# Context-by-weight products in f16 parts, with one power of two for a whole batch

## The reference

```
q  = layernorm(x)
t  = Wt @ ctx ; p = Wp @ q ; g = Wg @ ctx            (each 256 x 512)
att = sum over each of 8 groups of 32 channels of p * g, times 0.125
v  = groupnorm(Wz (att * t)) * gamma + beta + ctx
x1 = x + v
gate, up = fp4(layernorm(x1)) @ fp4(w_gate).T, ... @ fp4(w_up).T     (512 -> 1408)
out = x1 + fp4(silu(gate) * up) @ fp4(w_down).T
```

## Time and profile before

| what | us |
|---|---|
| median of 3 runs | 1733.88 |
| lowest and highest | 1733.24, 1734.05 |
| the profiled execution's own time | 1733.28 |
| its span in the profile | 1731.4 |
| PE busy | 1677.1 (97%) |
| DVE busy | 1501.5 (87%) |
| ACT busy | 825.9 (48%) |
| POOL busy | 722.5 (42%) |

### The profile page before, as it was taken

The page is one execution under the profiler, slowest core; times in us unless marked ns, Lnnn a source line. Parts: engine busy times, 40 slices in busy tenths (PEclk is TensorE's granted clock), DMA queues, the critical chain, the costliest instruction groups (busy, mean ns, idle before and its releaser), DMA issues.

```text
span 1731.4 us, 27880 instructions
## 1 busy us (share of the span) xinstructions
PE 1677.1 (97%) x8723; PEld 922.2 (53%) x8723; DVE 1501.5 (87%) x2577; ACT 825.9 (48%) x1472; POOL 722.5 (42%) x951
## 2 busy tenths in 40 slices
PE   2799999999999999999999999999999999999999
PEld 1665555555555555555555555555555555555544
DVE  7877888889888888988888898888888988888887
ACT  3665544544445444444545444454544445445422
POOL 7986343334444333444433334443333444433310
PEclk9999999999999999999999999999999999999999
DMA  8123334343434344343334434333434444343322
GB/s 258 34 43 81 83 91 95 88 100 89 95 81 94 89 91 99 88 106 76 88 89 100 94 85 104 76 89 91 103 88 94 95 82 92 91 94 88 76 50 49
DMA packets 412150, 155.86 MB, mean 90 GB/s; under 512 B 383200, under 2 KB 384480, under 8 KB 412128
## 3 DMA queue, kind: packets, MB, share of 16 engines
q1 hardware_dynamic: 396352, 125.17, 33.9%
q10 hardware_dynamic: 15776, 30.41, 5.5%
HBM read 43.03 MB, written 16.78 MB: 35 GB/s over the span
## 4 chain that ended last, share of the span: by engine, by line
PE 91%; POOL 6%; DVE 1%; DMA 1%; issue 1%; ACT 0%; SPq 0%; POOLq 0%; DVEq 0%; ACTq 0%
PE pairs L550 52%; PE work L561 26%; PE work L500 5%; PE work L512 3%; PE work L527 2%; PE ubank L527 2%; POOL raw L1864 2%; POOL raw L1853 1%; POOL w_parts L1864 1%; POOL w_parts L1853 1%; DMA raw<-in_L_ffn_w_gate 0%; DMA hT_parts<-raw 0%; POOL xc L1787 0%; PE pairs L580 0%; POOL q_parts L1803 0%
## 5 line engine op out<-in xcount | busy, mean ns | idle before, releaser
L550 PE MATMUL pairs<-w_gate_hi,xT_parts 128*128 128x512 f16 (+1 forms) x1536 | 555.1, 361 | 0.5 <-DMA xT_parts<-raw 0.5
L550 PE MATMUL pairs<-w_up_hi,xT_parts 128*128 128x512 f16 (+1 forms) x1536 | 554.7, 361 | 0.0
L561 PE MATMUL work<-w_parts,hT_parts 128*128 128x512 f16 x2079 | 458.9, 379 | 0.9 <-DMA hT_parts<-raw 0.9
L561 PEld LDWEIGHTS work<-w_parts,hT_parts 128*128 128x128 f16 x2079 | 203.5, 99 | 236.0 <-issue 1.1
L550 PE MATMUL pairs<-w_up_lo,xT_parts 128*128 128x512 f16 (+1 forms) x768 | 277.5, 361 | 0.0
L550 PE MATMUL pairs<-w_gate_lo,xT_parts 128*128 128x512 f16 (+1 forms) x768 | 277.4, 361 | 0.0
L550 PEld LDWEIGHTS pairs<-w_gate_hi,xT_parts 128*128 128x128 f16 x1536 | 152.7, 99 | 155.7 <-issue 8.2
L550 PEld LDWEIGHTS pairs<-w_up_hi,xT_parts 128*128 128x128 f16 x1536 | 150.3, 98 | 146.8
L964 ACT ACTIVATE early<-pairs,w_unit 128x512 f32<-128x512 f32 (+1 forms) x192 | 124.8, 650 | 163.2 <-PE pairs L550 163.2
L915 ACT ACTIVATE wm<-h 128x1408 bf16<-128x1408 f32 (+2 forms) x65 | 87.2, 1341 | 204.9 <-DVE h L1184 204.9
L873 ACT CAST raw<-hq 128x704 f16<-128x704 f32 x126 | 98.2, 779 | 180.0 <-DVE hq L1201 179.3
(11 more groups left out here) (193 smaller groups left out, 2801.7 us busy)
## 6 DMA issues: line engine op xcount, KB each, us to landing
out<-raw SPq DMA_DIRECT2D x64, 256.0 KB, 2.1
c_in<-in_ctx ACTq DMA_DIRECT2D x29, 512.0 KB, 3.8
x_in<-in_x ACTq DMA_DIRECT2D x29, 512.0 KB, 5.2
raw<-in_L_ffn_w_down SPq DMA_DIRECT2D x2, 1408.0 KB, 8.8
raw<-in_L_ffn_w_gate SPq DMA_DIRECT2D x2, 1280.0 KB, 8.5
w_parts<-in_L_ffn_w_up SPq DMA_DIRECT2D x2, 1280.0 KB, 9.2
x_in<-in_x SPq DMA_DIRECT2D x3, 512.0 KB, 4.1
c_in<-in_ctx SPq DMA_DIRECT2D x3, 512.0 KB, 4.7
```

Of the source, the lines that this page charges most:

```text
L550: mm = pe.matmul(pairs[:, pair, n, 0:b - a], xT[s][part][:, k, :], w1[n][wpart][:, k, a:b], start=(k == 0 and part == 0 and wpart == 0), s ...
L561: mm = pe.matmul(obank[:, :], hT[part][:, k, :], w2[wpart][:, k, :], start=(k == 0 and part == 0 and wpart == 0), stop=(k == KH - 1 and pa ...
```

## The change

The context gets one power of two for the whole batch in place of one for each row, so that the same f16 parts serve `gram` and `u_rows`; the 32-bit parts go, and the fused weight is split into f16 parts as well. The power of u is taken out in `copy_u`.

- `ctx_square` writes its squares to another buffer. The row sums go to DRAM (`save_rows`) and come back with all 256 of them on every partition (`spread_rows`), both issued by ACT. `ctx_peak` (DVE) takes their largest. For batch 0 the peak goes over TensorE (`attention_rows`, `attention_top`, `attention_spread`), together with that of the weight.
- `ctx_fit` makes four passes (f16 and f32 for each tile), `ctx_lo` (POOL) subtracts the f16 from the f32 and writes f16. `ctx_hi` and `ctx_fit_lo` go.
- `scale_of_u` (DVE) makes the factor for `copy_u`.
- In the body, ACT does `ctx_fit` behind `affine(i+1,0)`, DVE does `ctx_peak` behind `gated(j,0,1)` and `ctx_power` and `scale_of_u` behind `gated(j,0,2)` (before: `ctx_power` ahead of `gated(j,0,0)`), POOL does `ctx_root` behind `columns` and both `ctx_lo` behind `columns_affine`.

```diff
-        wuT = [sb(f"wuT_{part}", [P, HT, C], F32R) for part in ("hi", "lo")]
+        wuT = [sb(f"wuT_{part}", [P, HT, C], F16) for part in ("hi", "lo")]
@@ PE, u_rows
-                pe.wait_ge(c_ready, HT * b + HT)
+                pe.wait_ge(c_fit_ready, HT * b + HT)
-                        mm = pe.matmul(u_bank(b, s), wuT[wpart][:, k, s * P:(s + 1) * P], c_wide[part][:, k, :],
+                        mm = pe.matmul(u_bank(b, s), wuT[wpart][:, k, s * P:(s + 1) * P], c_parts[:, k, part, :],
@@ PE, before turn_weights(0)
             top_of_rows(0)
+            attention_rows()
             spread_top(0)
+            attention_spread()
@@ ACT
+                act.wait_ge(u_scale_made, b + 1)
+                nc.scalar.activation(u_sb[:, s, :], u_bank(b, s), ACT.Identity, scale=u_scale[:, 0:1],
...
+            def save_rows(b):
+                act.wait_ge(c_squared, HT * b + HT)
+                at_least(act, c_rows_spread, 16 * (b - 1))
+                nc.scalar.dma_start(c_rows, c_norm[:, 0, :]).then_inc(c_rows_saved, 16)
+            def spread_rows(b):
+                act.wait_ge(c_rows_saved, 16 * b)
+                at_least(act, c_peaked, b)
+                nc.scalar.dma_start(c_all[:], c_rows.rearrange("p h -> (p h)").unsqueeze(0).to_broadcast([P, HT * P])
+                                    ).then_inc(c_rows_spread, 16)
...
                 for s in range(HT):
                     nc.scalar.activation(c_parts[:, s, 0, :], c_in[:, s, :], ACT.Identity,
-                                         scale=c_norm[:, 2, s:s + 1]).then_inc(c_fit_done, 1)
+                                         scale=c_norm[:, 2, 0:1]).then_inc(c_fit_done, 1)
+                    nc.scalar.activation(c_scaled[:, s, :], c_in[:, s, :], ACT.Identity,
+                                         scale=c_norm[:, 2, 0:1]).then_inc(c_scaled_done, 1)
@@ ACT, body
                     ctx_square(i + 2)
+                    save_rows(i + 2)
                 h_hi(j - 1, 0)
                 h_hi(j - 1, 1)
                 silu_group(j, 0, 0)
+                if ahead:
+                    spread_rows(i + 2)
...
-                if ahead:
-                    ctx_fit(i + 2)
                 silu_group(j, 0, 1)
                 x_hi(j + 1)
-                if ahead:
-                    ctx_hi(i + 2)
                 silu_group(j, 0, 2)
                 if more:
                     affine(i + 1, 0)
                 if ahead:
-                    ctx_fit_lo(i + 2)
+                    ctx_fit(i + 2)
@@ DVE
+            def ctx_peak(b):
+                if isinstance(b, int) and b == 0:
+                    dve.wait_ge(att_spread, 1)
+                    nc.vector.tensor_copy(c_norm[:, 1, 1:2], mixed_bank(0)[:, 1:2]).then_inc(c_peaked, 1)
+                    return
+                dve.wait_ge(c_rows_spread, 16 * b)
+                at_least(dve, c_floored, b)
+                nc.vector.tensor_reduce(c_norm[:, 1, 1:2], c_all[:, :], AX_X, ALU.max).then_inc(c_peaked, 1)
@@ DVE, start: order
+            attention_peak()
             weight_top(0)
+            attention_top()
             weight_max(1, 0)
             normalise1(0, 1)
             weight_unit(0)
+            ctx_peak(0)
+            weight_max(1, 1)
             ctx_power(0)
...
             copy_group(0)
+            ctx_peak(1)
             ctx_power(1)
@@ DVE, body
                     ln1_moments(i + 2, 0)
-                    ctx_power(i + 2)
                 gated(j, 0, 0)
...
                 gated(j, 0, 1)
                 if ahead:
+                    ctx_peak(i + 2)
                     ln1_moments(i + 2, 1)
...
                 gated(j, 0, 2)
+                if ahead:
+                    ctx_power(i + 2)
+                    scale_of_u(i + 2)
                 h_first(j)
@@ POOL
-                pool.wait_ge(c_squared, HT * b + HT)
+                pool.wait_ge(c_peaked, b + 1)
...
-                nc.gpsimd.tensor_tensor(c_wide[1][:, s, :], c_in[:, s, :], c_wide[0][:, s, :].bitcast(F32),
-                                        ALU.subtract).then_inc(c_ready, 1)
+                nc.gpsimd.tensor_tensor(c_parts[:, s, 1, :], c_scaled[:, s, :], c_parts[:, s, 0, :],
+                                        ALU.subtract).then_inc(c_fit_ready, 1)
@@ POOL, body
+                columns(i + 1)
                 if ahead:
                     ctx_root(i + 2)
-                columns(i + 1)
+                columns_affine(i + 1)
                 if ahead:
                     ctx_lo(i + 2, 0)
-                columns_affine(i + 1)
-                if ahead:
                     ctx_lo(i + 2, 1)
```

More of the change, by code:

```diff
@@ L137, in build @@
         cT = sb("cT", [P, HT, 2, KD, P], F16)
-        c_wide = [sb(f"c_{part}", [P, HT, D], F32R) for part in ("hi", "lo")]
+        c_scaled = sb("c_scaled", [P, HT, D])
+        c_all = sb("c_all", [P, HT * P])
+        u_scale = sb("u_scale", [P, 1])
         c_norm = sb("c_norm", [P, 4, HT])
@@ L620, in spread_top, with attention_rows, attention_spread @@
                           stop=True).then_inc(w_allmax_done, 1)
+            def attention_rows():
+                pe.wait_ge(wu_peaked, 1)
+                pe.wait_ge(c_squared, HT)
+                for n, column in enumerate((wu_pow[:, 0:1], c_norm[:, 0, 0:1], c_norm[:, 0, 1:2])):
+                    mm = pe.matmul(mixed_bank(0)[0:1, n * P:(n + 1) * P], column, ident[:, :], start=True, stop=True)
+                mm.then_inc(att_rows_done, 1)
+            def attention_spread():
+                pe.wait_ge(att_top_done, 2)
+                pe.matmul(mixed_bank(0)[:, 0:2], ones_row[:, :], att_top[:, 0:2], start=True,
+                          stop=True).then_inc(att_spread, 1)
             def unit_read(m):
@@ L886, in ctx_fit @@
                 at_least(act, gram_done, b)
+                at_least(act, c_turned, 16 * b)
+                at_least(act, u_done, HT * b)
+                act.wait_ge(c_squared, HT * b + HT)
                 for s in range(HT):
                     nc.scalar.activation(c_parts[:, s, 0, :], c_in[:, s, :], ACT.Identity,
[L889 to L904 removed]
+                                         scale=c_norm[:, 2, 0:1]).then_inc(c_fit_done, 1)
+                    nc.scalar.activation(c_scaled[:, s, :], c_in[:, s, :], ACT.Identity,
+                                         scale=c_norm[:, 2, 0:1]).then_inc(c_scaled_done, 1)
             def q_hi(b):
@@ L993, in _ @@
             ctx_square(1)
+            save_rows(1)
             weights_lo(0)
             weights_lo(1)
+            spread_rows(1)
             weights_hi(2)
@@ L1025, in _ @@
             weights_hi(11)
-            ctx_hi(1)
             weights_hi(12)
@@ L1049, in _ @@
             weights_hi(19)
-            ctx_fit_lo(1)
             weight_grain(9)
@@ L1088, in _ @@
             ctx_square(2)
+            save_rows(2)
             affine(1, 0)
+            spread_rows(2)
             weights_lo(31)
@@ L1099, in _ @@
             ctx_fit(2)
-            ctx_hi(2)
             q_hi(2)
@@ L1103, in _ @@
             grain_x(2)
-            ctx_fit_lo(2)
             silu_group(1, 1, 2)
@@ L1497, in _ @@
             weight_unit(0)
+            ctx_peak(0)
+            weight_max(1, 1)
             ctx_power(0)
-            weight_max(1, 1)
+            attention_parts()
+            scale_of_u(0)
             weight_round(0)
+            attention_lo()
             weight_scales(1, 0)
@@ L1517, in _ @@
             variance(0)
+            scale_of_u(1)
             ln1_moments(1, 1)
@@ L1586, in _ @@
             h_lo(0, 0)
+            ctx_peak(2)
             ctx_power(2)
+            scale_of_u(2)
             x_scales(2)
```

98 lines of the change are left out of this document (67 added, 31 removed).

## The result

The changed kernel takes **1769.93 us** (median of 6 runs, 1768.74 to 1771.30) against 1733.97 of the kernel before on the same chip (6 runs, 1733.24 to 1734.93). The ratio is 1.0209, with an interval of 1.0198 to 1.0220. The forecast was 1771.6. Every time here is the median of the executions at the usual granted clock, 0.996 to 0.999; the one execution that fell to 0.756 (2224.82 us, in run 4) is left out. The profiled execution took 1770.55 with a span of 1768.5 us, 37.1 more than the 1731.4 before.

A forecast was written before the change was run, and what follows sets the result against it. PE's own work was taken to bound the loop, the POOL chain the part before it. Loop +32.5, last body -0.3 and start +5.5 gave +37.7 on the median 1733.9: 1771.6 us, range 1738 to 1798.

The forecast's parts named there:

- the loop: 29 rounds that prepare a batch ahead: PE stall less saved matmul time, net +1.12 us a round, 32.5 us.
- the start: Before the loop: POOL waits 3.3 us for the first peak, 2.2 more for the second; 5.5 us, from 2 to 8.
- The PE work that goes: Twelve u matmuls a batch at L527 with f16 operands: 0.33 us saved a batch, bounds 0.20 to 0.42.
- a switch less on the way into L550: Behind the u matmuls on PE: one switch fewer, counted into the 0.33 us saved a batch.
- The shift of DVE: DVE's chain to `gated(j+1,1,0)`: 1.8 us later at 808.5 through added instructions and `ctx_lo` port collisions, bounds 0.3 to 2.6.
- The stall of PE: PE in each loop round: waits 1.8 - 0.35 = 1.45 us for DVE's late results.
- both named deadlines: PE's `hidden(j+1,1,2)` needs `gated(j+1,1,0)`, room 0.5 us; `output(j)` needs h's transpose, room 0.35 us.
- The trip through DRAM: ACT's `save_rows` and `spread_rows`: 2.1 us to landing, no wait; taken as zero, other end 1 us a round.
- Rival (c): `save_rows` lands over 4 us after issue, ACT's chain moves, up to 1 us more a round: 1800; chance 0.05.
- (a): Port costs DVE's chain nothing, shift under 0.35 us, the matmul saving stays: 1729.5 or 1726; chance 0.13.
- (b): Only one `ctx_lo` collides; shift about 0.8 us, PE waits 0.45 a round: 1743; chance 0.12.
- (d): f16 u matmuls no faster than the old form, stalls as forecast, 9.9 us more: 1781; chance 0.03 within the forecast's range.

The follow-up runs named there:

- run 4: Kernel before the change, only the u product taking f16 operands, the scaling left out and squares in another buffer: 1726.59 us, ratio 0.9958.
- run 2: Changed kernel in its own order; in the loop POOL's `ctx_lo` subtracts 2 columns instead of 512: 1736.98 us, ratio 1.0016 to the kernel before.
- run 3: Kernel before the change, only `ctx_hi` moved behind `affine(i+1,0)` and `ctx_lo(0)` behind `columns_affine`, no instruction added: 1757.52 us, ratio 1.0133.
- run 11: Changed kernel with early context passes in the loop and three reorderings before it, measured once more on another chip: 1731.35 us, ratio 0.9988.
- Run 7: Changed kernel with early context passes in the loop, and ACT's `ctx_fit(1)` split into two pairs behind `weights_lo(8)`: 1735.52 us, ratio 1.0007.
- run 8: Changed kernel, early context passes; before the loop `ctx_peak(1)`, `weight_max(1,0)`, `ctx_peak(0)` earlier on DVE and `ctx_fit(1)` split on ACT: 1730.89 us, ratio 0.9983.
- run 1: Changed kernel, loop reordered: `ctx_fit` ahead of `silu_group(j,0,2)`, both `ctx_lo` ahead of `columns_affine`, root, peak and power passes earlier: 1737.11 us, ratio 1.0018.

## Why the prediction was right, and where it was not

The sign, the place and the mechanism held, and the time came out 1.7 us from the forecast. But that closeness is owed to two errors of opposite sign: the loop was forecast at 32.5 us and cost 29 x 0.946 = 27.4; the start was forecast at 5.5 and cost 37.1 - 27.4 + 0.1 = 9.8.

**The PE work that goes: 0.22 us a batch, not 0.33.** The pitch of 0.2155 was right. What failed is the step "the first takes 0.42 us because its 32-bit weight load lies open behind the L512 ones". The 0.19 us at the first matmul are gone, but the 32-bit block ahead grew by 0.18 us, though its operands are the same; why, no run shows. The 0.03 us for "a switch less on the way into L550" had no row behind it and did not show either. Only the difference of pitch was saved, near the stated lower bound of 0.20. Run 4 gives the same 0.22. Read from the u block alone, the saving would be 0.40; only both blocks together, from the start of the one ahead, show what PE gained.

**The shift of DVE: 1.56 us, not 1.8.** Run 2 and run 3 show the port as its cause, one by taking it away in the changed kernel, the other by putting it into the kernel before. By its pieces: +0.39 for the small instructions (forecast 0.48), -0.7 for the first scaling, +0.94 for the second, +0.96 for `residual`. The order of the collisions was the other one that the text named, "if `h_y` gets in first, `ctx_lo(1)` blocks `residual` behind it and the delay is the same". It is nearly the same. The Trainium skill, "SBUF — State Buffer", section "Who interferes with whom", says that the loser is blocked for the whole instruction; the rows agree (1.21 and 1.64 us where 0.27 and 0.68 stood, beside a pass of 1.16). Run 3 adds that POOL's second pass may take the port right behind its first, ahead of the DVE instruction that is due. There ACT had both inputs ready early, here it finished the second pass's only at 819.40; whether that decides the order was not tested.

**The stall of PE: 1.17 us, not 1.45**, at both named deadlines, in the order named, with the room as worked out: 1.56 - 0.35 = 1.21. So the error is nearly all the shift's. The period of 51.3 came out at 51.15.

**The trip through DRAM: 2.9 us to landing, not 2.1.** The fastest of 31 took 2.5 us, the slowest 4.1. "At 2.1 us `spread_rows` waits for nothing" came out in most rounds even so, since ACT is busy until then; in 11 rounds it waits 0.6 to 1.9 us. Rival (c) asked for a landing over 4 us, which one round reached. Its price would not have come either: run 11 waits for the trip in 22 rounds, 21.8 us in all, and PE has no gap in the loop. ACT had the room behind it. The likeness was badly chosen. The store of `out` is large, but the trip's 1 KB goes out as 128 pieces of 8 bytes behind two loads of 512 KB on ACT's queue, and the trace does not part the one cause from the other. The some 2.0 us of fixed cost that the prediction takes from the Trainium skill, "DMA: Bandwidth & Descriptors", section "Anatomy of one DMA", stand there for DMAs that GpSimd issues; this one is ACT's, and its measured 2.9 us decide.

**The start: two of the three terms measured as forecast, and one left out.** `ctx_root(0)` came 3.4 us late (3.3 forecast) and `ctx_root(1)` 5.3 us late (3.3 + 2.2). What was missing is ACT. The text counted ACT "lighter by about 1.3 us a round" and worth nothing, which holds in the loop. But before the loop `ctx_fit(1)` is a block of 2.45 us (four passes) where one pair of 1.3 us stood, right ahead of a conversion that PE waits for, and the cover that "PE waits anyway" gives there is no cover for ACT. PE's wait there grew by 1.2 us, from 3.65 to 4.87. Run 7 gains 1.9 us by its move, from two ratios that are good to 1.6 us each; what goes beyond the 1.2 would be part of a wait that the kernel before had too. At the second gram the delay is 7.4 us (127.51 against 120.07), so some 0.9 us between the second `ctx_root` and it (7.4 - 5.3 - 1.2) has no cause shown. Another 2.4 us (9.8 - 7.4) comes with batch 2 and the first round, where 0.5 was forecast. The changed kernel has the two waits for h's transposes that run 8 has, 1.20 us at 169.96 and 1.58 us at 222.53; the second holds part of the steady loss as well.

Of the rivals, (a) asked for a DVE shift under 0.35 us, which runs 1 and 2 bring about by other means, and then its loop came out but for the smaller saving. (b) needed one collision only; there were two. (d) falls with run 4. The range was drawn with a stall of 0.8 to 2.1 us, narrower than the prediction's own bounds of the shift (0.3 to 2.6 us, less 0.35 of room); at the measured 1.17 the difference plays no part.

**A version a little shorter than both** is run 8: the change with the early passes and the three start moves, 1730.9 and 1731.35 us in two measurements, 0.9983 and 0.9988 of the kernel before, both intervals under 1. The gain is 2 to 3 us, about what the prediction said that a measurement tells (0.2%), as the product's 6.6 us are partly spent on a start that is still 3.9 us longer.

## What to carry to other kernels

When a pass on POOL moves, list what DVE does in that stretch, which of it reads two tensors in SBUF, and which was stretched beside POOL before, like the one-input scaling here: the duration of either in the old place is not its duration in the new one, and a chain with 0.35 us of room pays for it every round. When the order in a loop is set by hand, a change is not one verdict but a verdict and a placement; ask for the last moment at which each new piece is needed, and here, too, the first possible one: the two passes run some 6 us earlier in run 1, and cost nothing there. And when a sum comes out right, check its terms one by one: this one had two errors of 4 and 5 us that hid each other.

## What was not expected of the hardware

- A block of 32-bit matmuls before an f16 one took 1.72 us, and before another 32-bit one 1.54, with the same operands; what the first matmul behind it lost in time showed up in the block ahead.
- A one-input instruction of DVE over 88 columns is blocked by a POOL pass of two inputs (0.27 becomes 1.21 us), as the prediction had read from 0.88 us before; but its moments pass over 512 columns and its one-column instructions ran beside one at their usual length (run 1, 0.69 us), and so did `gated(j,0,2)`, one of whose tensors is in PSUM (0.62 us).
- With POOL passes of 2 columns (0.20 us, 0.62 beside `h_y`) in the same places the loop had no gap in PE (run 2). So it is the length of the pass beside the chain that costs, not the handing over of the port.
- 1 KB in 8-byte pieces to DRAM took 2.9 us to landing in the median (2.5 to 4.1), and 128 KB back, spread to 128 partitions, 4.0 us.
- The transpose of h took 5.2 us to landing in the loop, and 6.8 to 7.0 in some places around its start: one of the first five in the kernel before (issued at 183.53), three in run 8.
